# A graph network kernel on one core: TensorE's register loads of window offsets, taken for up to three edge groups at once

## The reference, cut to what matters

```python
W = jnp.zeros((1024, 1024)).at[src, dst].add(edge_weight)
x = x + relu(layernorm(x)) @ W.T + L0_gnn_bias
h0 = relu(layernorm(x))
agg(h) = segment_sum(h[src], dst, 1250) * deg_inv[:, None]
h1 = relu(h0 @ W_self0 + agg(h0) @ W_neigh0 + b0)
x = x + h1 @ W_self1 + agg(h1) @ W_neigh1 + b1
```

## Time and profile before

| | |
|---|---|
| timed executions | 776.11, 776.92 (median), 778.68 us |
| profiled execution | 778.68 us, of which the span of instructions is 777.0 us |
| TensorE matmul busy | 750.0 us, 97% of the span, 4433 matmuls |
| VectorE, ScalarE, GpSimd busy | 574.9 (74%), 356.1 (46%), 479.0 (62%) us |
| mean granted TensorE clock | 0.998 |
| build on TensorE | from about 12.6 to 83.9 us of the span |

### The profile page before, as it was taken

How to read it: one execution, slowest core, us unless ns; L and a number is a source line. 1 busy time by engine, 2 the same in 40 slices (tenths; PEclk the granted TensorE clock), 3 DMA queues, 4 the chain that set the end, 5 groups by cost and what they waited for, 6 DMA issues and landing times.

```text
span 777.0 us, 13499 instructions
## 1 busy us (share of the span) xinstructions
PE 750.0 (97%) x4433; PEld 620.0 (80%) x4434; DVE 574.9 (74%) x813; ACT 356.1 (46%) x596; POOL 479.0 (62%) x593
## 2 busy tenths in 40 slices
PE   3899999999999999999999999999999999999998
PEld 2777888888778888888888888888888888887886
DVE  7999587678455799975758685446397957679896
ACT  7877634334244267733326655543222324344731
POOL 5000265766758899777747282327699966745982
PEclk9999999999999999999999999999999999999999
DMA  3122467675376763585864625786754667885475
GB/s 115 43 79 92 125 191 228 203 254 179 122 266 196 269 217 94 167 262 187 291 220 134 202 95 174 218 254 229 248 163 129 219 197 274 280 273 184 149 235 198
DMA packets 82873, 148.78 MB, mean 191 GB/s; under 512 B 10795, under 2 KB 20898, under 8 KB 82800
## 3 DMA queue, kind: packets, MB, share of 16 engines
q1 hardware_dynamic: 62862, 105.07, 42.6%
q10 hardware_dynamic: 19938, 42.79, 15.6%
HBM read 106.42 MB, written 41.41 MB: 190 GB/s over the span
## 4 chain that ended last, share of the span: by engine, by line
PE 85%; POOL 4%; issue 4%; DVE 4%; ACT 2%; DMA 0%; POOLq 0%; ACTq 0%; DVEq 0%
PE bank L1703 44%; PE bank L1753 21%; PE bank L1637 12%; PE bank L1539 3%; PE bank L1534 1%; PE bank L1555 1%; POOL T L1114 1%; PE bank L1769 1%; ACT asum L1278 1%; PE bank L1630 1%; POOL S L1081 1%; PE bank L1550 1%; POOL split L1099 1%; POOL narrow L1041 1%; DVE L L1936 1%
## 5 line engine op out<-in xcount | busy, mean ns | idle before, releaser
L1703 PE MATMUL bank<-slot,split 128*128 128x512 f32 x1128 | 263.2, 392 | 2.7 <-issue 2.7
L1703 PEld LDWEIGHTS bank<-slot,split 128*128 128x128 f32 x1128 | 211.9, 189 | 46.8 <-issue 3.1
L1061 POOL TENSOR_TENSOR AT<-AT,az 128x50 int32 (+3 forms) x288 | 96.8, 336 | 116.7 <-DMA az<-asum_scratch 72.3
L1703 PE MATMUL bank<-slot,split_third 128*128 128x512 f32 x552 | 129.6, 390 | 0.5 <-DVE cst L2302 0.3
L1703 PEld LDWEIGHTS bank<-slot,split_third 128*128 128x128 f32 x552 | 103.1, 188 | 22.3 <-issue 0.6
L1753 PE MATMUL bank<-slot,Ax 128*128 128x512 f32 x500 | 118.9, 392 | 0.2
L2073 DVE TENSOR_TENSOR slot<-T,slot 128x512 fp32r<-128x512 f32 x64 | 85.7, 1357 | 33.4 <-ACT slot L1319 30.8
L1753 PEld LDWEIGHTS bank<-slot,Ax 128*128 128x128 f32 x500 | 92.8, 188 | 20.3 <-issue 1.4
L1637 PE MATMUL bank<-slot,split_m 128*128 128x512 f32 x320 | 91.2, 396 | 0.0
L1116 POOL TENSOR_TENSOR T<-T,wst 128x512 f32<-128x512 f32 x48 | 67.9, 1432 | 1.4 <-DMA wst<-in_L_gnn_W_self 1.4
L1637 PEld LDWEIGHTS bank<-slot,split_m 128*128 128x128 f32 x320 | 58.5, 188 | 11.1
(11 more groups left out here) (229 smaller groups left out, 1220.3 us busy)
## 6 DMA issues: line engine op xcount, KB each, us to landing
stage<-hT_scratch SPq DMA_DIRECT2D x90, 256.0 KB, 3.7
wst<-in_L_gnn_W_neigh SPq DMA_DIRECT2D x56, 256.0 KB, 4.7
wst<-in_L_gnn_W_self SPq DMA_DIRECT2D x56, 256.0 KB, 3.3
x1b_scratch<-x ACTq DMA_DIRECT2D x10, 512.0 KB, 5.9
hT_scratch<-hTs ACTq DMA_DIRECT2D x10, 512.0 KB, 3.1
wst<-prod0g_scratch SPq DMA_DIRECT2D x20, 256.0 KB, 3.1
hT_scratch<-h1s ACTq DMA_DIRECT2D x20, 256.0 KB, 3.3
wst<-prod1g_scratch SPq DMA_DIRECT2D x20, 256.0 KB, 3.5
```

Source lines behind the costliest of these rows:

```text
L1061: pool.tensor_tensor(a, a, az32[:, n % NZ, pairs * pos:pairs * (pos + 1)], ALU.add) \
L1703: last = pe.matmul(dense_bank(v, which)[:, :], split_tile(v, a)[:, NT * k:NT * (k + 1)], slot[t % 2][:, b, HF * (HK * which + k):HF * (HK ...
```

## The change

The offsets of up to three groups (24 words, `AT_ONCE`) come in one register load, taken ahead of the first of them; a load never mixes groups that have different numbers of offsets. The words that are read are now spaced by `SHARED[j]`, so that shared windows take one word each. This gives loads ahead of groups 0 (2 words), 2 (2 words), 3 (12 words), 6, 9, 12, 15, 18, 21, 24, 27, 30, 33 (24 words each) and 36 (8 words). The bases come in four loads of 4, 8, 16 and 5 words, ahead of groups 3, 8, 15 and 31; where both are loaded ahead of one group, the offsets come first, as before. The order of all other instructions is as it was.

```diff
+AT_ONCE = 24
-BASES = {3: range(4, 8), 4: range(8, 16), 5: range(16, 24), 6: range(24, 32), 25: range(32, LATE)}
+BASES = {3: range(4, 8), 8: range(8, 16), 15: range(16, 32), 31: range(32, LATE)}
...
-                        last = pe.matmul(w_bank(j)[:, bass.ds(offsets[c - c % SHARED[j]], kw(j))], row,
+                        last = pe.matmul(w_bank(j)[:, bass.ds(offsets[c // SHARED[j]], kw(j))], row,
...
             def load_offsets(j):
-                at = GC * j
-                return load(pe, tab_o[0:1, at:at + 1 if SHARED[j] == GC else at + GC], 0, (WW - WD) * TW)
+                each = GC // SHARED[j]
+                upto = j + 1
+                while upto < LATE and SHARED[upto] == SHARED[j] and each * (upto + 1 - j) <= AT_ONCE:
+                    upto += 1
+                values = load(pe, tab_o[0:1, GC * j:GC * upto:SHARED[j]], 0, (WW - WD) * TW)
+                offsets_of.update((n, values[each * (n - j):each * (n - j + 1)]) for n in range(j, upto))
...
-                offsets = load_offsets(j)
+                if j not in offsets_of:
+                    load_offsets(j)
                 if j in BASES:
                     ...
+                offsets = offsets_of[j]
                 pe.wait_ge(s_R, j + 1)
                 pe.wait_ge(s_L, j + 1)
                 column_sums(j)
```

More of the change, by code:

```diff
@@ L1569, in spread_mean @@
                 pe.matmul(mean_bank(i), all_ones[:, :], mean[:, i % 2, :], start=True, stop=True).then_inc(s_t0, 1)
-            base_of = {}
+            offsets_of, base_of = {}, {}
             def load_offsets(j):
-                at = GC * j
-                return load(pe, tab_o[0:1, at:at + 1 if SHARED[j] == GC else at + GC], 0, (WW - WD) * TW)
+                each = GC // SHARED[j]
[4 more added lines that the diff above has]
+                offsets_of.update((n, values[each * (n - j):each * (n - j + 1)]) for n in range(j, upto))
             for j in range(LATE):
```

## The result

The changed kernel takes **783.29 us** (median of 6; 779.43 to 786.63) against **775.86 us** before (median of 6; 773.85 to 778.68). The ratio is 1.0101, 95% interval [1.0070, 1.0132]: about 7.4 us slower. Sixteen more executions of the changed kernel lay between 780.4 and 788.0. The prediction was 777.2 us, with a range up to 780.2. It was wrong, and most of its steps can be checked one by one.

What follows compares the result with a forecast made beforehand. TensorE's sequencer, a third of it register loads, was taken to pace the build; 1.1 + 0.1 - 0.28 - 0.28 - 1.12 + 0.17 + 0.55 = +0.24, taken as +0.3 on 776.92, gave 777.2 us, range 774.4 to 780.2.

Steps and rivals of the forecast that it cites:

- 18 to 20 and 21 to 23: the sequencer's pace, -0.28 each: Build, these two triples: TensorE's sequencer sets the pace, so one load of 24 for three of 8 saves 0.28 us each.
- 24 to 26: Build, this triple: -0.28 us, and with the base load ahead of group 25 gone, -1.12 us.
- The lead of 17 matmuls: TensorE's queue in the build: the sequencer can issue at most 17 matmuls ahead of the array, hiding part of a load.
- The price of a load: TensorE's register loads: words cost, not instructions; 24 words take 1.61 us, bounds 1.50 and 1.86.
- Groups 27 to 29: Build, windows of 10: the array stands 0.74 us at a load; 5.93 us against 5.76, +0.17.
- groups 30 to 32: Build: +0.15 us as in the triple before, about +0.4 from the 5 bases ahead of group 31; together +0.55.
- Groups 0 to 17: Build's start: group 12 at 34.0 instead of 34.34, group 15 at 41.5 instead of 40.44 (+1.1 us), 15 to 17 +0.1.
- A shift of group 36 should reach the end nearly whole: Behind the build: GpSimd's chain and TensorE's path both start from group 36, so its +0.3 us passes to the end.
- Rival 1: Build's loads: price per instruction, hardly per word; group 36 5.2 us early, 771.7 us; chance 0.09.
- Rival 2: Load ahead of group 3: spaced words cost a fetch each, 3.8 us instead of 0.85; total +2.4, 779.3 us; chance 0.13.
- Rival 3: TensorE's queue in the build: the lead is 32 pairs, no stall of 0.74; -1.1 us, 775.8 us; chance 0.11.
- Rival 4: Long stall ahead of group 15: rise to 2.4 GHz comes two groups later, +0.8 to +1.3 us; 778.3 us; chance 0.12.

Runs made afterwards that it cites:

- ninth run: Changed kernel, but groups 27 to 35 take group 26's offset values again, leaving out the loads ahead of 27, 30 and 33: 779.79 us, ratio 1.0058.
- fourth run: Changed kernel with five matmuls of 512 columns on zeros ahead of each load of 24 from group 12 on: 783.09 us, ratio 1.0096.
- unused loads: Kernel before, meant to get 14 extra register loads at three places, but nothing used their values and they were not in its program: 775.82 us.
- bases early: Kernel before with the last five bases loaded ahead of group 6 instead of group 25: 775.30 us, ratio 1.0003.
- bases alone: Kernel before with only the base loads changed (4, 8, 16, 5 words ahead of groups 3, 8, 15, 31): 779.12 us, ratio 1.0038.
- n = 5: Kernel before with 5 matmuls of 512 columns on zeros ahead of group 33, no load touched (a plain delay): 776.19 us, ratio 1.0014.
- the pair cut before and after: VectorE's sums of blocks 38 and 39 done over 64 of 512 columns, in the kernel before (774.41 us) and in the changed kernel (780.79 us).
- twelfth run: Kernel before with 14 extra register loads of various sizes and spacings ahead of groups 2, 20 and 33, each value used once; no whole-kernel time given.
- values reused: The ninth run: changed kernel with group 26's offset values used again for groups 27 to 35: 779.79 us, ratio 1.0058.
- fifteenth run: Sums of blocks 38 and 39 cut to 64 columns; kernel before (774.41 us) or that with 11 zero matmuls ahead of group 33 (781.57); text doesn't say which.
- thirteenth: Changed kernel with VectorE's sums of blocks 38 and 39 done over 64 of 512 columns: 780.79 us, ratio 1.0084.

## Why the prediction was wrong

**The failed step: "18 to 20 and 21 to 23: the sequencer's pace, -0.28 each", and 24 to 26 with it.** I had taken 1.27 us as what a group needs between loads and let the sequencer alone set it. The sequencer did pace the kernel before. But take the loads away and the array is next: groups 24 and 25 of the changed kernel have no load behind them and take 1.66 and 1.49 (62.47 - 60.81, 63.96 - 62.47). Three groups cost 3 x 1.5 and what a load lasts beyond the matmuls that are already issued. (In the ninth run, groups 22 and 25, with no load ahead or behind, took 1.49 each.) I used this very sum from group 27 on and not here. The change's three triples from 18 to 26 took 18.45 us where I had 16.54, so 1.9 of the miss. Even with the load at 1.61, the triple of 21 to 23 (6.18 us) would have been 6.18 - 0.42 = 5.76, where it was 5.84 before: next to nothing to gain from the start.

**The lead of 17 matmuls.** It was never reached here. At the load of 58.61 six matmuls were still to start, 0.4 us of work; at those of groups 30 and 33, 14 and 12 (0.7 and 0.6, where I had 1.03). The sequencer gains only about 0.1 to 0.2 us a group of windows of 8 on the array (an estimate, 1.5 less the 1.27 taken from the earlier trace rows), so the lead stays small; 17 is an upper limit, which only the earlier trace rows reached. The short loads before cost the array 0.43 us each (groups 20 to 22 took 5.77 in the profile of before, less 3 x 1.49), three of them 1.3; the long one behind group 23 cost it 1.7 (6.18 less 3 x 1.49).

**The price of a load.** 1.61 was right for a load by itself (1.62) and too low where DMA traffic ran beside it (2.00 to 2.03, outside my bounds): 0.4 for each of the five from 52.4 on, contained in the misses of the triples. Groups 27 to 29 lost 0.74 (predicted 0.17), groups 30 to 32 1.00 (0.55), groups 33 to 35 nothing, as predicted.

**Groups 0 to 17.** Group 12 started at 35.26, predicted 34.0; group 15 at 41.81, predicted 41.5. That the second is so near is luck: group 12 was 1.3 late, and groups 12 to 14 then ran through the array at a granted clock of 1.00, faster than I had reckoned, and stood waiting for the two loads (2.37 us idle). I had called the slow pace of these groups in the kernel before the 1.2 GHz level; the profile's granted clock reads 1.00 there, although the starts are as far apart (0.17 us a chunk) as in the changed kernel's stretch at 0.51. So the level of that stretch is not shown by its row. Groups 15 to 17 lost 1.45 where I had 0.1: part goes with the low clock from 40.9 to 47.8 (0.5 less in the fourth run, which is also filled), the rest is the same missing term as above. The sum of the measured steps is 1.37 + 1.45 + 0.23 + 0.74 + 1.00 + 0.01 = 4.80.

**"A shift of group 36 should reach the end nearly whole"** failed too. Set against the medians, the profile's delay makes 4.8 of the 7.4 us, and 2.6 more come from behind the build. From the first dense matmul to the last, the six profiles without a stall or a low clock there (the unused loads, bases early, bases alone, n = 5, and the pair cut before and after) took 555.9 to 556.8 us; the changed kernel's took 563.6, with 3.0 for the wait near 330, about 3 for the low clock and 0.8 for a wait at 303.9. Of the 6.1 us between the forecast and the median, 4.5 are thus the build and 2.6 what is behind it, less 1.1 by which the median of the kernel before came out lower (775.86 against 776.92).

**The rivals.** Rival 1 (a price per instruction) is refuted by the twelfth run. The Trainium skill's floor for a `tensor_load`, about 600 ns ("DMA: Bandwidth & Descriptors", Latency and other measured facts), doesn't hold there either: 4 words took 0.338, and the measurement decides. Rival 2 had the mechanism (0.235 us a spaced word, over its threshold of 0.13) and part of the size: without the spaced words the delay fell by 1.6 us, where it had 2.1. But group 6 was already back to 0.08 us late against the kernel before, most of the delay arose later, and the time hardly fell. Rival 3 is refuted: at every load behind which groups 21 to 36 began, 14 matmuls or fewer were still to start. Rival 4 has its low clock, ahead of group 18 and not of group 15; with the clock held high (fourth run), groups 15 to 17 took 0.5 us less and group 36 came no earlier.

**What stays open.** Why a delay of 2.5 to 5 us costs 2.6 to 5 more than itself, and one of 5.5 or 9.4 only 0.5 and 1.7 (medians against those of the kernel before beside them, each uncertain by some 2 us); and why, at a delay of 1, the kernels with changed loads lost 3 to 4 us more than the plain delay: with most of the late end taken away (values reused), 5.2 us of loss are left. The profiles show two places where the extra appears, the wait for GpSimd before the dense products and VectorE's pair near 330, each at times with a low clock behind it. GpSimd's chain of additions, 118.6 to 127.1 us from the first addition to the first split in different profiles, decides the first; what makes it vary was not tried. No version was shown to beat the kernel before.

## What to carry to other kernels

Merging register loads saves little when words have the price: 24 at once took 1.62 to 2.03 us, three times 8 take 1.77, and the one load stands in one piece, which the work already issued must cover. Before taking away the pace-setter, work out what the next one needs, for every stage. And in a kernel at 97% TensorE, judge an edit by the time of many executions: here a delay of 1.2 us cost 1.2 and one of 2.5 cost 6.8.

## What the runs showed of the hardware

- TensorE's register loads, by themselves (twelfth run): 0.31 us for 1 word, 0.54 for 2, 0.34 for 4 (0.57 and 0.36 at two other places), 0.59 for 8, 0.85 for 12, 1.11 for 16, 1.62 for 24; spaced words 0.54 for 2, 0.99 for 4, 1.93 for 8, 2.86 for 12.
- A load of 24 words took 1.61 to 1.63 us where the DMA engines were at most 5% busy during it, and 1.86 to 2.04 where they were 34 to 42% busy (63 loads in seven profiles). The granted clock does not sort them: it was 0.50 to 1.00 at the first and 1.00 at the second.
- A VectorE sum of two SBUF tiles over 512 columns took 0.68 us in GpSimd's pauses and up to 1.79 beside its work; over 64 columns 0.22 in a pause (fifteenth run), and 1.04 and 1.34 beside it (thirteenth). The extra is the same for both sizes: 0.82 and 1.12 for 64 columns, 0.80 and 1.07 for 512 (1.48 and 1.75 in the changed kernel). That fits a sum that waits for the other engine's instruction and doesn't share with it. The Trainium skill ("SBUF — State Buffer", Terms) says that VectorE and GpSimd take the shared port pair exclusively, for a full instruction, and that the loser blocks. The trace agrees, with GpSimd's instructions of 1.3 us there.
